# A ring of three PSUM slots in a selective scan: the product of the next state ahead of each scan

## What is computed

```
delta = softplus(dt_w @ dts + dt_b)
h[n]  = exp(delta * A[n]) * h[n] + (delta * u) * B[n]      # along the 2,304 pixels
y     = sum over n of h[n] * C[n]  + D * u
```

## Time and profile before

| | |
|---|---|
| median of 3 runs | 32,617.53 us (32,604.29 to 32,618.05) |
| the profiled execution | 32,605.19 us, its span 32,603.4 us |
| VectorE busy | 28,731.8 us, 88% of the span |
| TensorE busy | 24,387.7 us, 75% |
| GpSimd busy | 22,314.8 us, 68% |
| ScalarE busy | 15,872.9 us, 49% |
| mean granted clock of TensorE | 0.909 |

### The profile page before, as it was taken

One profiled execution on the slowest core, in us unless ns is written; L12 is line 12 of the kernel. 1 busy time (PEld: TensorE's weight loads), 2 busy tenths in 40 slices (PEclk: granted clock), 3 DMA queues, 4 the chain that ended last, 5 costly groups with the idle time before them and its releaser, 6 DMA issues.

```text
span 32603.4 us, 317462 instructions
## 1 busy us (share of the span) xinstructions
PE 24387.7 (75%) x78148; PEld 12020.4 (37%) x78148; DVE 28731.8 (88%) x21480; ACT 15872.9 (49%) x22789; POOL 22314.8 (68%) x12356
## 2 busy tenths in 40 slices
PE   7777777777777777777777777777777777777777
PEld 3333333333333333333333333333333333333333
DVE  8888998899888998889988898888898888988888
ACT  5444454445444454444544454444454444544444
POOL 7666766667666776667766676666676666766666
PEclk9888988899888998889889998899999889989999
DMA  4333433334333333334333343333343333433333
GB/s 133 105 106 104 133 114 106 105 110 137 106 106 104 120 127 105 106 105 133 114 103 112 109 140 118 112 112 113 121 135 112 112 112 109 139 118 112 112 113 121
DMA packets 1409449, 3759.43 MB, mean 115 GB/s; under 512 B 204384, under 2 KB 204512, under 8 KB 1404896
## 3 DMA queue, kind: packets, MB, share of 16 engines
q1 hardware_dynamic: 1407328, 3736.27, 35.2%
HBM read 3659.95 MB, written 47.19 MB: 114 GB/s over the span
## 4 chain that ended last, share of the span: by engine, by line
issue 47%; DVE 36%; PE 13%; ACT 2%; POOL 2%; DVEq 1%; DMA 0%; SPq 0%; POOLq 0%; ACTq 0%
DVE ps L1153 23%; DVE arena L487 5%; DVE arena L1157 4%; PE ps L673 3%; PE ps L577 1%; PE ps L827 1%; PE ps L826 1%; PE ps L661 1%; PE ps L645 1%; PE ps L622 1%; POOL arena L1295 1%; DVEq L1155 1%; PE ps L814 0%; PE ps L815 0%; DVE arena L484 0%
## 5 line engine op out<-in xcount | busy, mean ns | idle before, releaser
L1295 POOL TENSOR_TENSOR arena<-arena 128x768 f32<-128x768 f32 x9216 | 16682.3, 1813 | 5310.9 <-DVE arena L1157 4937.5
L673 PE MATMUL ps<-arena,consts 128*128 128x384 f32 x36864 | 14075.2, 506 | 369.4 <-ACT arena L1007 190.5
L1157 DVE TENSOR_TENSOR_SCAN arena<-arena,carry,ps 128x768 f32<-128x768 f32 x6144 | 11143.7, 1814 | 672.7 <-DVE ps L1153 33.8
L954 ACT ACTIVATE arena<-arena,An 128x768 f32<-128x768 f32 x9216 | 8578.1, 934 | 4428.8 <-POOL arena L1295 3674.3
L661 PE MATMUL ps<-arena,consts_b 96*128 96x512 bf16 (+1 forms) x18432 | 4751.7, 341 | 6201.4 <-DVE arena L1157 5993.0
L1153 DVE TENSOR_TENSOR ps<-ps,arena 128x768 f32<-128x768 f32 x9216 | 8681.6, 942 | 251.1 <-PE ps L661 246.5
L673 PEld LDWEIGHTS ps<-arena,consts 128*128 128x128 f32 x36864 | 6477.1, 196 | 4750.1 <-issue 571.7
L1157 DVE TENSOR_TENSOR_SCAN arena<-arena,ps 128x768 f32<-128x768 f32 x3072 | 5387.3, 1754 | 348.7 <-ACT arena L954 30.7
L661 PEld LDWEIGHTS ps<-arena,consts_b 96*128 96x128 bf16 x18432 | 1312.6, 100 | 11433.8 <-DVE arena L1157 10183.1
L984 ACT COPY carry<-arena 128x1 f32<-128x1 f32 x6144 | 1166.6, 190 | 6130.9 <-DVE arena L1157 6129.8
L487 DVE SCALAR_TENSOR_TENSOR arena<-arena,wp 128x2304 f32<-128x2304 f32 (+1 forms) x896 | 2332.3, 2603 | 31.6
(11 more groups left out here) (157 smaller groups left out, 18671.1 us busy)
## 6 DMA issues: line engine op xcount, KB each, us to landing
arena<-c_rows SPq DMA_DIRECT2D x6144, 384.0 KB, 3.5
arena<-c_rows SPq DMA_DIRECT2D x6144, 192.0 KB, 3.3
arena<-arena SPq DMA_DIRECT2D x384, 72.0 KB, 2.0
c_rows<-arena SPq DMA_DIRECT2D x32, 576.0 KB, 4.5
arena<-x SPq DMA_DIRECT2D x17, 864.0 KB, 4.3
arena<-mid SPq DMA_DIRECT2D x17, 864.0 KB, 4.4
mid<-arena SPq DMA_DIRECT2D x16, 864.0 KB, 4.7
out<-arena SPq DMA_DIRECT2D x16, 864.0 KB, 4.1
```

Of the source, the lines that this page charges most:

```text
L673: mm = pe.matmul(y_part[:, h, :], ident, hC[it % NW][:, h * SEG:(h + 1) * SEG], start=(n == 0), stop=(n == NS - 1))
L954: act.activation(state_at[it % NW], delta[g % 2], ACT.Exp, scale=An[:, slot(s) * NS + n:slot(s) * NS + n + 1]).then_inc(sem["da_ready"], 1)
L1157: dve.tensor_tensor_scan(a[:, ::back], a[:, ::back], slots[it % 2][:, ::back], 0.0 if k == 0 else carry[:, n:n + 1], ALU.mult, ALU.add).th ...
L1295: pool.tensor_tensor(hC[it % NW], state_at[it % NW], Csb[b], ALU.mult).then_inc(sem["hc_ready"], 1)
```

## The change

The three pairs of banks 2 to 7 become one ring of three slots. The B products of all states, the step-size units (`pre_delta`) and the second units take their slots in this ring in the order in which TensorE issues them. `slot_uses` writes that order down once: which use has which place, and which semaphore count frees it. A use waits until the use three places earlier is freed (`slot_freed`).

VectorE issues the product of state it + 1 ahead of scan it (`input_term`), except where a unit stands between the two states in the ring (`crowded`: after state 1, and after state 9 where there is a second unit). There the product comes after the scan, together with the following one.

`pre_delta` moves from after state 3 to after state 1. The steps of ScalarE and GpSimd that hang on it move forward by one to three states, the second unit's copy from state 13 to 11, its gate multiply from 13 to 9, `move_sums` and `gate_sums` from 4 to 3.

```
+PRE_AFTER, SECOND_AFTER = 1, 9
+def crowded(it):
+    g, n = it // NS, it % NS
+    return n == PRE_AFTER and g + 1 < NG or n == SECOND_AFTER and second_unit(g) is not None
+def slot_uses():
+    freed, place = [("pre_taken", 1)], {("pre", 0): 0}
+    for g in range(NG):
+        for n in range(NS):
+            place["b", NS * g + n] = len(freed)
+            freed.append(("scanned", NS * g + n + 1))
+            if n == PRE_AFTER and g + 1 < NG:
+                place["pre", g + 1] = len(freed)
+                freed.append(("pre_taken", g + 2))
+            if n == SECOND_AFTER and second_unit(g):
+                place["second", g] = len(freed)
+                freed.append(second_unit(g))
+    return freed, place
-        SLOT_AT = (4 * BANK, 2 * BANK)
+        SLOT_AT = (6 * BANK, 4 * BANK, 2 * BANK)
...
             def in_proj_z(i):
-                pe.wait_ge(sem["pre_taken"], v("pre_taken", i + 2))
+                slot_freed("second", i)
...
             def merge_columns(c):
-                pe.wait_ge(sem["pre_taken"], v("pre_taken", FIRST_MERGE + c + 2))
+                slot_freed("second", FIRST_MERGE + c)
...
             def pre_delta(g):
-                    pe.wait_ge(sem["pre_taken"], v("pre_taken", g))
+                    slot_freed("pre", g)
...
+            def slot_freed(kind, k):
+                name, n = FREED[PLACE[kind, k] - 3]
+                pe.wait_ge(sem[name], v(name, n))
...
             def broadcast(g, n):
-                    pe.wait_ge(sem["scanned"], v("scanned", it - 1))
+                    slot_freed("b", it)
...
             def scan(g):                                  # TensorE
-                    if n == 3 and g + 1 < NG:
+                    if n == PRE_AFTER and g + 1 < NG:
                         pre_delta(g + 1)
...
             def scan(g):                                  # ScalarE
-                    if n == 4 and g > 0:
+                    if n == 3 and g > 0:
                         move_sums(g - 1)
                     if g + 1 < NG:
+                        if n == 2:
+                            evacuate(g + 1)
+                        if n == 4:
+                            exp_part(g + 1)
                         if n == 5:
-                            evacuate(g + 1)
+                            plus_one(g + 1)
+                        if n == 6:
+                            log_part(g + 1)
                         if n == 7:
-                            exp_part(g + 1)
-                        if n == 8:
-                            plus_one(g + 1)
-                        if n == 9:
-                            log_part(g + 1)
-                        if n == 10:
                             less_one(g + 1)
-                    if n == 13:
+                    if n == 11:
...
+            def input_term(it):
+                g, n = it // NS, it % NS
+                if n == 0:
+                    dve.wait_ge(sem["du_ready"], v("du_ready", g + 1))
+                dve.wait_ge(sem["b_bcast"], v("b_bcast", it + 1))
+                dve.tensor_tensor(b_slot(it), b_slot(it), du[g % 2], ALU.mult).then_inc(sem["dbu_ready"], 1)
...
             def scan(g):                                  # VectorE
                     it = NS * g + n
-                    if n == 0:
-                        dve.wait_ge(sem["du_ready"], v("du_ready", g + 1))
-                    dve.wait_ge(sem["b_bcast"], v("b_bcast", it + 1))
-                    dve.tensor_tensor(slots[it % 2], slots[it % 2], du[g % 2], ALU.mult).then_inc(sem["dbu_ready"], 1)
+                    if it == 0 or crowded(it - 1):
+                        input_term(it)
+                    if it + 1 < NIT and not crowded(it):
+                        input_term(it + 1)
...
-                    if At.layer == 0 and n == 4 and g > NG - NC:
+                    if At.layer == 0 and n == 3 and g > NG - NC:
                         gate_sums(g - 1)
-                    if At.layer == 0 and n == 13 and 0 <= g - FIRST_MERGE < NC:
+                    if At.layer == 0 and n == 9 and 0 <= g - FIRST_MERGE < NC:
                         gate_merged(g - FIRST_MERGE)
...
             def scan(g):                                  # GpSimd
+                        if n == 6:
+                            rounded_off(g + 1)
                         if n == 8:
-                            rounded_off(g + 1)
+                            log1p(g + 1)
                         if n == 10:
-                            log1p(g + 1)
+                            add_relu(g + 1)
                         if n == 12:
-                            add_relu(g + 1)
-                        if n == 13:
                             times_input(g + 1)
```

More of the change, by code:

```diff
@@ L84, with second_unit @@
 GATES_AT = 2 * NC
+PRE_AFTER, SECOND_AFTER = 1, 9
+def second_unit(g):
+    if g < len(Z_UNITS):
+        return "z_copied", g + 1
+    if 0 <= g - FIRST_MERGE < NC:
+        return "merge_taken", g - FIRST_MERGE + 1
+    return None
+def crowded(it):
[14 more added lines that the diff above has]
+    return freed, place
+FREED, PLACE = slot_uses()
 COMMON = [("w_in", 448), ("w_xa", 3 * XA), ("w_xb", 3 * NBC), ("w_dt", PAIRS * 3 * P),
@@ L244, in tok, with b_slot, unit_slot @@
                 "p (i d) -> p i d", d=DM) for g, n in ((0, 5), (1, 4))]
-        slots = [ps[:, at:at + CH] for at in SLOT_AT]
+        def b_slot(it):
+            at = SLOT_AT[PLACE["b", it] % 3]
+            return ps[:, at:at + CH]
+        def unit_slot(kind, g):
+            at = SLOT_AT[PLACE[kind, g] % 3]
+            return ps[:, at:at + 2 * BANK].rearrange("p (g x) -> p g x", x=BANK)[:, :, 0:SEG]
         y_part = ps[:, Y_AT:Y_AT + 2 * BANK].rearrange("p (g x) -> p g x", x=BANK)[:, :, 0:SEG]
-        pre_part = ps[:, PRE_AT:PRE_AT + 2 * BANK].rearrange("p (g x) -> p g x", x=BANK)[:, :, 0:SEG]
         def halves(a):
@@ L610, in in_proj_z @@
                     at = c * CH + h * SEG
-                    mm = pe.matmul(pre_part[0:m, h, :], wcol("w_in")[0:DM, (2 + t) * P:(2 + t) * P + m], xT[:, at:at + SEG],
+                    mm = pe.matmul(unit_slot("second", i)[0:m, h, :], wcol("w_in")[0:DM, (2 + t) * P:(2 + t) * P + m], xT[:, at:at + SEG],
                                    start=True, stop=True)
@@ L615, in merge_columns @@
             def merge_columns(c):
-                pe.wait_ge(sem["pre_taken"], v("pre_taken", FIRST_MERGE + c + 2))
+                part = unit_slot("second", FIRST_MERGE + c)
+                slot_freed("second", FIRST_MERGE + c)
                 hold(pe)
@@ L620, in merge_columns @@
                     at, r = c * CH + h * SEG, (2 * c + h) * SEGROWS
-                    pe.matmul(pre_part[0:DB, h, :], ident[:, 0:DB], u[1][:, at:at + SEG], start=True, stop=False)
-                    mm = pe.matmul(pre_part[0:DB, h, :], ident[:, DB:P], by_column(u[1])[:, r:r + SEGROWS, :],
+                    pe.matmul(part[0:DB, h, :], ident[:, 0:DB], u[1][:, at:at + SEG], start=True, stop=False)
+                    mm = pe.matmul(part[0:DB, h, :], ident[:, DB:P], by_column(u[1])[:, r:r + SEGROWS, :],
                                    start=False, stop=True)
@@ L644, in pre_delta @@
                     at = c * CH + h * SEG
-                    mm = pe.matmul(pre_part[:, h, :], w[rows, p, j, :], xa[rows, at:at + SEG], start=True, stop=True)
+                    mm = pe.matmul(unit_slot("pre", g)[:, h, :], w[rows, p, j, :], xa[rows, at:at + SEG], start=True, stop=True)
                 mm.then_inc(sem["pre_ready"], 1)
+            def slot_freed(kind, k):
+                name, n = FREED[PLACE[kind, k] - 3]
+                pe.wait_ge(sem[name], v(name, n))
             def broadcast(g, n):
@@ L989, in copy_z @@
                 act.wait_ge(sem["z_ready"], v("z_ready", i + 1))
-                act.copy(halves(chunk(sz[t], c))[0:m, :, :], pre_part[0:m, :, :]).then_inc(sem["z_copied"], 1)
+                act.copy(halves(chunk(sz[t], c))[0:m, :, :], unit_slot("second", i)[0:m, :, :]).then_inc(sem["z_copied"], 1)
             def gates():
@@ L998, in move_merged @@
                 act.wait_ge(sem["merge_ready"], v("merge_ready", c + 1))
-                act.copy(halves(chunk(yg[1], c)), pre_part[0:DB, :, :]).then_inc(sem["merge_taken"], 1)
+                act.copy(halves(chunk(yg[1], c)), unit_slot("second", FIRST_MERGE + c)[0:DB, :, :]).then_inc(sem["merge_taken"], 1)
             def move_sums(g):
@@ L1174, in gate_merged @@
                 dve.wait_ge(sem["merge_ready"], v("merge_ready", c + 1))
-                dve.tensor_tensor(halves(chunk(yg[1], c)), pre_part[0:DB, :, :], halves(chunk(sz[1][0:DB, :], c)), ALU.mult)\
+                dve.tensor_tensor(halves(chunk(yg[1], c)), unit_slot("second", FIRST_MERGE + c)[0:DB, :, :],
+                                  halves(chunk(sz[1][0:DB, :], c)), ALU.mult)\
                     .then_inc(sem["merge_taken"], 1)
```

18 lines of the change are left out of this document (6 added, 12 removed).

## The result

The changed kernel takes 33,189 us (median of 4 runs, 33,163 to 33,205) against 32,618 us. The ratio is 1.0174, interval 1.0156 to 1.0192: 1.7% slower, where 2.4% faster was forecast. The profiled execution has a span of 33,203.5 us, 600 us more than that of before.

What follows compares the result with a forecast made beforehand. The prediction took VectorE to set the pace. Its terms, 32,605 - 1,580 - 127 + 705 + 198 + 26 = 31,827, gave a forecast of 31,830 us, 2.4% faster, with a range of 31,080 to 32,480 us.

Steps and rivals of the forecast that it cites:

- (a): VectorE's product runs one state ahead, so the gap before each scan goes and an overlap replaces it: 1,580 us gained.
- (b): TensorE's B broadcasts wait for a scan one state earlier and are used one earlier: 1.62 us needed of 2.60, hidden.
- (c): Step-size units (`pre_delta`) in the ring: low clock behind 8 in 10 of 544 delays products by 1.62 us, 705 us lost.
- (d): Second units in the ring: z units hidden with no clock fall, merges delay products 10 and 11, 198 us lost.
- (e) to (g): `gate_sums`' 119 us of waits stay, another 127 us go; the sums' extra matmuls lose 26 us; GpSimd's moved steps stay hidden.
- the clock falls at every unit: Rival: TensorE's clock falls at z and merge units too, each following 2.1 us of idling; 32,470 us, chance 0.13.

Runs made afterwards that it cites:

- experiment 5: kernel 3 with the product taken back to directly before its own scan: 32,342 us, ratio 0.9919 to the kernel before.
- kernel 3: The changed kernel with the sum issued ahead of the unit and step-size matmuls over 108 rows instead of 12: 30,905 us, ratio 0.9474.
- experiment 1: The changed kernel with TensorE issuing the sum (`add_state`) ahead of the unit at each crowded place: 31,107 us, ratio 0.9538.
- 4: The changed kernel with seven extra 128-column matmuls before the unit at each crowded place but those of group 0: 31,362 us, ratio 0.9614.
- experiment 7: The kernel before with the step-size unit waiting for the scan of state 2, and the sum ahead of both units: 32,661 us, ratio 1.0015.
- 6: The kernel before with one added wait, the step-size unit waiting for the scan of state 2: 34,483 us, ratio 1.0575.
- experiment 2: The changed kernel with step-size matmuls over 108 rows instead of 12, the added rows' weights zero: 32,665 us, ratio 1.0017.
- 9: The kernel before with step-size matmuls over 108 rows: 32,526 us, ratio 0.9974.

## Why the prediction was wrong

By its own steps:

- **(a) the product-ahead** was right in mechanism and close in size: 1,580 us forecast, 993 + 760 = 1,753 us measured, and 1,437 us net in experiment 5. The overlap is 0.09 us where rows 4 gave 0.07, and the scans' durations are 13 ns shorter. The Trainium skill's page "VectorE: DVE Perf Modes", section "The DRAIN you can't avoid", says that the next instruction waits until the pipeline is empty and that a semaphore costs nothing extra. It adds that a next instruction that is not held starts earlier, which the prediction left out. The traces show the difference: the dependent scan started 0.11 us after the product's end, the independent one starts 0.09 before it. Experiment 5 differs from kernel 3 by that order alone.
- **(b) the broadcasts' slot** was right: in ordinary states a product doesn't wait for TensorE; it does at the places of the table alone.
- **(c) the step-size units: this step failed.** It gave 705 us; the waits behind these units are 1,482 us. Two errors stand in it. It took the low clock to begin behind the unit, as in the earlier trace rows, and so priced the unit at its high-clock 1.48 us. That holds at 53 of 512 places, and there the price is right (1.59 us against 1.62). At the other 459 the low clock covers most or all of the unit; it occupies 2.83 us in the timeline above. With that difference of 1.35 the price is 1.62 + 1.35 = 2.97, and the timeline has 2.95. And the share was more than the 8 in 10: in groups 1 to 16, of which a run has 512, product 2 waits 510 times and product 3 512 times. The argument saw the idle gap of 2.1 us and used it only to raise a frequency that came from units without such a gap.
- **(d) the second units: failed for z, close for the merges.** The z units were taken as free, and cost 455 us. The evidence was one gap of 1.84 us with a high clock behind it; one row couldn't bear that. The merges cost 276 us where 198 were forecast, 234 at the products and 42 at the gate multiply, which the step took to fill a part of the wait and which waits itself.
- **(e) to (g)**: `gate_sums` costs 122 us, 118 before. The extra matmuls cost 39 us at product 15 (26 forecast) and 81 at product 13, which was not foreseen. GpSimd's steps are hidden, as forecast.
- **Missing from the sum**: the start of each image. Product 5 of group 0 waits 101 us in all for a chain that begins with the DMA of the first C row. No exchange in TensorE's queue helps there (100 us in experiment 1).

The forecast's own sum, corrected: 31,827 + 777 for (c) + 455 for z + 101 for the images' start + 81 and 13 for the extra matmuls + 78 for the merges - 173 for (a) = 33,159. Another 20 us are old waits that stayed or grew, and 28 us of idle time stand in front of other instructions. That comes to 33,207; the profiled execution took 33,205. The rival "the clock falls at every unit" named the right event, with a chance of 0.13. It gave 32,470 us, because it used the same price of 1.62 us.

What the experiments show of the cause: without the idle gap of some 2.1 us in front of the unit, the clock is high through every step-size unit behind it (544 of 544 in experiments 1 and 4), and the time is back (1 and 4 against the changed kernel, 7 against 6). The gap is not the whole of it. In front of the z units it is the same in the changed kernel and in experiments 2 and 7, and yet 181, 109 and 37 of the 192 units have a granted clock below 0.6. That the rows of the step-size matmuls count is shown by the gains of 524, 202 and 90 us of experiments 2, 3 and 9. How they reach the z units, eight states later, is open; that the z units also gain in experiment 7, where the rows stay 12 and the step-size units run at the high clock, says only that what went before the gap matters.

## What to carry to other kernels

A wait that is moved in an in-order queue has two prices: what stands behind it, and what the engine's clock does while it idles. In TensorE's queue put independent work in front of the waiting item, not behind it; exchanging two items of the queue was worth 2,082 us here, more than the idea that the change was made for. When a step is priced at a low clock, ask whether the step itself or only its followers run at it, and take a frequency only from places with the same idle time in front. Even these need the same work before the gap.

An in-order VectorE with a product and a dependent scan gains about 0.2 us per pair when the next pair's product stands between them.

## What the runs showed of the hardware

- An idle gap of 2.16 us in front of a unit was followed by a fall of the granted clock from 1.00 to 0.50 at all 512 step-size places of the changed kernel. At 328 of them the clock was down when the unit started, at the others it fell during the unit or behind it. The same gap in front of the z units left the clock high over the unit (0.95 or more on average) at 58 of 192 places in experiment 7 and at 79 of 192 in experiment 2.
- With the sum in the gap (at most 0.82 us of idling left in front of a step-size unit, 0.87 in front of a z unit) the clock was high through all 544 and all 192 of them (experiment 1).
- Matmuls on 12 rows are followed by low clock more often than the same matmuls on 108 rows, and the unit itself takes about as long (808 against 812 ns in the changed kernel, 522 in both with the sum first): the mean of the sums' matmuls fell from 506 to 491 ns in the kernel before and from 506 to 496 ns with the sum first.
- Adding 10,752 matmul records to TensorE made its busy time shorter, 25,829.5 to 25,225.0 us, and the kernel 1,827 us faster.
- On VectorE a scan that waits for the product just before it starts 0.11 us after that product's end; a scan behind a product that it doesn't depend on starts 0.09 us before the end.
